# A decoder layer on one core: the second attention of batch 0 moved eight steps later in a written plan

## The reference

```python
x = x + attn(layernorm(x))      # 16 heads of 8, scores + q.rel_emb_k[clip(j-i)], softmax, .(v + rel_emb_v[...])
x = x + xattn(ctx, layernorm(x))  # shifts the sequence by 32 (and by 8), appends ctx and a strided convolution
x = x + ffn(layernorm(x))
# ffn(src): q, k, v (k and v through a rank of 32), rope on q and k, softmax attention, Wo,
#   rmsnorm; a shared SwiGLU MLP of 256, and 8 experts in 2 groups, the best 2 of the best group, gated;
#   out = rmsnorm(x + shared + routed)
```

## Time and profile before

| what | value |
|---|---|
| time, 3 runs | 451.37, 451.47, 452.81 us (median 451.47) |
| the profiled execution | 455.62 us, span 453.8 us |
| mean granted TensorE clock | 0.874 |
| busy PE | 387.8 us (85%) |
| busy DVE | 289.3 us (64%) |
| busy ACT | 236.0 us (52%) |
| busy POOL | 167.7 us (37%) |

### The profile page before, as it was taken

One profiled execution on the slowest core, in us unless ns is written; L12 is line 12 of the kernel. 1 busy time (PEld: TensorE's weight loads), 2 busy tenths in 40 slices (PEclk: granted clock), 3 DMA queues, 4 the chain that ended last, 5 costly groups with the idle time before them and its releaser, 6 DMA issues.

```text
span 453.8 us, 14631 instructions
## 1 busy us (share of the span) xinstructions
PE 387.8 (85%) x6148; PEld 228.1 (50%) x6163; DVE 289.3 (64%) x518; ACT 236.0 (52%) x494; POOL 167.7 (37%) x347
## 2 busy tenths in 40 slices
PE   5967887999999989898988887989788888987973
PEld 5411354666767667565455545544355454543431
DVE  3744765676687778878388878555877820353445
ACT  1533366576667676666652665476157768212200
POOL 5540044454677666474451132120025100013462
PEclk9975555698999999999999968879858988998989
DMA  7300000000000000100003200000000000000000
GB/s 235 100 1 10 13 3 4 4 5 21 6 4 6 6 4 9 26 5 2 3 4 85 72 13 12 2 2 1 2 1 2 5 2 3 0 1 12 0 12 24
DMA packets 12078, 8.19 MB, mean 18 GB/s; under 512 B 4558, under 2 KB 11102, under 8 KB 11886
## 3 DMA queue, kind: packets, MB, share of 16 engines
q1 hardware_dynamic: 12014, 7.27, 5.6%
HBM read 5.94 MB, written 0.52 MB: 14 GB/s over the span
## 4 chain that ended last, share of the span: by engine, by line
PE 57%; DVE 18%; ACT 7%; issue 7%; POOL 5%; SPq 3%; DMA 2%; ACTq 0%; POOLq 0%; DVEq 0%
PE ps L1086 10%; DVE m_qk L808 8%; PE ps L1063 7%; PE ps L1000 7%; PE ps L1019 6%; PE ps L1104 5%; PE ps L1049 5%; ACT arena L656 5%; PE ps L1194 4%; PE ps L1180 4%; PE ps L1159 2%; PE ps L925 2%; SPq L364 2%; PE ps L1110 2%; POOL rstd L413 1%
## 5 line engine op out<-in xcount | busy, mean ns | idle before, releaser
L808 DVE TENSOR_REDUCE m_qk<-ps 128x2 f32<-128x1024 f32 x128 | 153.3, 1219 | 43.1 <-PE ps L1019 42.3
L656 ACT ACTIVATE arena<-ps 128x512 f32<-128x512 f32 x256 | 139.0, 596 | 66.0 <-PE ps L1063 64.7
L1086 PE MATMUL ps<-arena,v_sb 128*20 128x128 f32 x2048 | 84.9, 295 | 0.0
L578 POOL TENSOR_TENSOR arena<-arena,eb 128x256 f32<-128x256 f32 x64 | 47.3, 739 | 63.4 <-ACT arena L656 33.1
L1063 PE MATMUL ps<-q_op,k_op 62*128 62x128 bf16 (+1 forms) x1024 | 56.8, 235 | 14.6 <-ACT arena L656 9.0
L1019 PE MATMUL ps<-k_op,q_op 48*128 48x512 bf16 x256 | 57.2, 443 | 8.2 <-DVE m_qk L808 6.5
L1063 PEld LDWEIGHTS ps<-q_op,k_op 62*128 62x128 bf16 (+1 forms) x1024 | 39.6, 102 | 41.5 <-ACT arena L656 21.0
L1086 PEld LDWEIGHTS ps<-arena,v_sb 128*20 128x20 f32 x2048 | 50.3, 104 | 18.5 <-issue 6.3
L412 POOL TENSOR_SCALAR var<-mv 128x4 f32<-128x4 f32 (+1 forms) x16 | 3.2, 201 | 114.9 <-ACT eb L718 62.9
L643 ACT ACTIVATE eb<-ps 128x512 f32<-128x512 f32 (+1 forms) x64 | 31.3, 541 | 27.1 <-PE ps L1049 26.9
L1000 PE MATMUL ps<-part,sel 32*128 32x512 bf16 x192 | 34.1, 471 | 8.2 <-issue 2.0
(11 more groups left out here) (200 smaller groups left out, 474.3 us busy)
## 6 DMA issues: line engine op xcount, KB each, us to landing
rel_v<-in_relv_ext SPq DMA_DIRECT2D x1, 1024.0 KB, 8.8
eb<-in_w SPq DMA_DIRECT2D x2, 512.0 KB, 6.2
x_sb<-in_x SPq DMA_DIRECT2D x2, 256.0 KB, 3.2
q_op<-farT SPq DMA_DIRECT2D x32, 3.0 KB
q_op<-farT SPq DMA_DIRECT2D x32, 1.5 KB
out<-x_sb SPq DMA_DIRECT2D x8, 64.0 KB, 1.5
rows<-in_rows SPq DMA_DIRECT2D x1, 448.0 KB, 6.6
sel<-in_sel SPq DMA_DIRECT2D x1, 384.0 KB, 4.2
```

The costliest lines, as they stand in the source:

```text
L578: pool.tensor_tensor(on0, on0, eb0[u % 2][:, p], ALU.mult)
L656: act.activation(p_ring[:, k % SLOTS_P, e, :], ps[:, bank, :], ACT.Exp).then_inc(sm["bank_free"], 1)
L808: dve.tensor_reduce(m_qk[:, u % NT, n:H:PAIRS], ps[:, banks, :], AX_X, ALU.max).then_inc(sm["pair_free"], 1)
L1086: i = pe.matmul(out, v_sb[:, IT * b + jt, 4 * g + hh, :], rhs, start=(g == 0 and jt == 0), stop=(u >= NT and jt == IT - 1), skip_group_che ...
```

## The change

Only numbers of the plan change. The four tiles of the second attention of batch 0 begin at 113, 122, 131, 140 and not at 105, 115, 125, 134; those of batch 1 one later each, at 153, 162, 171, 180. `y2` of batch 0 goes from 161.5 to 167.5, that of batch 1 from 206.5 to 207.5. The gate of batch 0 goes from 167 to 173, its two exponentials from 169 and 173 to 175 and 179, and `LAST` from 198.6 to 199.6. The middle stages (`MID_AT` 78 and 126) and `again` stay. No operation is added or removed.

```diff
 MID_AT = (78, 126)
-AGAIN_AT = (105, 115, 125, 134, 152, 161, 170, 179)
-FRONT_AT = (161.5, 206.5)
-LAST = 198.6
+AGAIN_AT = (113, 122, 131, 140, 153, 162, 171, 180)
+FRONT_AT = (167.5, 207.5)
+LAST = 199.6
...
-    plan += [(167, 5, "gate", 0, 0), (169, 5, "group_exp", 0, 0), (173, 5, "expert_exp", 0, 0)]
+    plan += [(173, 5, "gate", 0, 0), (175, 5, "group_exp", 0, 0), (179, 5, "expert_exp", 0, 0)]
```

## The result

The changed kernel is slower: median 469.9 us of four runs (467.4 to 471.3) against 452.1 for the kernel before (451.4 to 453.8), ratio 1.038 [1.032, 1.044]. The forecast was 449.2 with 445 to 454.5; direction and range are wrong. Single runs of any of these kernels differ by some per cent with the clock they got, so every ratio here leaves out the runs that are over some 1.5% longer than the fastest of their kernel, while medians go over all runs.

A forecast was written before the change was run, and what follows sets the result against it. PE was taken as the bound in all stretches but D, where DVE bounds; -2.2 + 3.0 - 1.0 + 0.5 - 2.6 = -2.3 us, or -0.5%, made the median 449.2, range 445 to 454.5.

The forecast's parts named there:

- A: From the end of `again` of batch 0 to `y` of batch 1: fewer maxima there, -2.2 us.
- The allowance of 1.5: In A: 1.5 us charged for a fall of the clock, out of up to 3.4, against a gain of 3.7.
- B: From `y` of batch 1 to its first `again`: four maxima and a `fin` come in on DVE, +3.0 us.
- the 43 to 45: Sign that B is right: the first `again` of batch 1 comes 43 to 45 us behind `y`.
- rival 4: Late shift DMAs make PE wait at `scores` of tile 9: 1 to 2 us, 451; chance inside two other rivals'.
- DVE without a gap over 1 in the last 12: Sign for B: DVE has no gap over 1 us in the last 12 us before the first `again`.
- C: First to last `again` of batch 1: moved `scores` and `pv` fill PE's idle place, clock stays up, -1.0 us.
- D: From the last `again` of batch 1 to `qk_rows` of tile 12: maxima bound by DVE, +0.5 us.
- E: From `qk_rows` of tile 12 to that of tile 13: at full clock 13.3 us instead of 17.14, -3.8.
- F: From `qk_rows` of tile 13 to the first `mlp` of batch 0: takes over `xT` and the gate, +1.2 us.
- Rival 2: Slower, 24%: PE starved between `back` of tile 6 and `y` of batch 1, clock stays low into B; +3.2, 454.7.

The follow-up runs named there:

- the filled hole: The changed kernel with 12 dense filler matmuls on PE ahead of the last maximum of tile 11, where PE idled 3.0 us: 459.4 us, ratio 1.013.

## Why the prediction was wrong

**A, right in size, in part by luck.** -2.15 for -2.2. `back` of tile 6 started at 238.86 behind 2.08 us of PE idle (worked out: 239.5 behind some 2.3). `y` started at 256.37; all of A begins 0.65 earlier here, so that is 1.5 later than the 255.5 worked out without clock loss. The allowance of 1.5 fits, and the clock did fall, at 239.5 for 3.4 us with PE busy in all of them and again at 253. But only the first of the two falls seems to cost A anything. In three other profiles with this order of A the second one is longer, and A takes 28.0 at a clock of 0.83 or 0.84; here and in a fourth it takes 28.2 and 28.3 at 0.88. Where the first one is 6.8 long and not 3.4 (the filled hole), A takes 28.9. How much of the 1.5 is clock and how much DVE, which is busy for 20.2 of A, no run tells.

```profile
238.86 0.33 PE L1118 MATMUL ps<-ident,xn 128*128 128x128 f32 x1 [2.08 <-DVE xn L844]
256.37 2.08 PE L1137 MATMUL ps<-w_out,xnT 128*128 128x128 f32 x8
271.77 0.40 PE L1063 MATMUL ps<-q_op,k_op 50*128 50x128 bf16 x8 [2.49 <-DMA q_op<-neg_mT]
```

**B, right in kind, 1.1 short.** +4.1 for +3.0, within its high end of +4.5: the first `again` 45.1 behind `y`, just past the 43 to 45. The shift DMAs did what the earlier trace rows gave: the rows of tile 9 release `scores` 15.4 behind `y` (estimated 15.1), and PE waits 2.49 there, under the 3 that would have been rival 4. From `y` to DVE's first projection operation it took 31.5, where it had 31.6; the whole growth stands behind that, as forecast, and it isn't the clock, which is 0.88 over B where it was 0.83. But the mark "DVE without a gap over 1 in the last 12" failed:

```profile
293.17 1.22 DVE L808 TENSOR_REDUCE m_qk<-ps 128x2 f32<-128x1024 f32 x1
296.95 1.21 DVE L323 TENSOR_TENSOR rest<-part 128x512 f32<-128x512 f32 x1 [1.43 <-ACT part L696]
```

I had filled DVE's idle time with the maxima as if their order were free. It is a queue: DVE waits for ACT with a maximum ready behind it.

**C, the step that failed.** The step was "the moved `scores` and `pv` of tile 10 now fill that place", for -1.0, with +1.1 as the worst if the clock stays as it was. The place wasn't filled: the idle time ahead of the first `again` grew from 1.96, which is 1.65 without the missing matmul, to 3.00, with another 1.15 just ahead of it. I counted the work that moves in and not the wait of PE that the queue on DVE makes (the pair of `max`, behind the split, behind ACT). And I bounded a fall by the one seen, 6.8 us; it was 37.4. The worst case stood in no bound of mine, and the rows had it: 15.0 busy with 6.3 of it at half clock is 11.9 at full clock, 13.0 with the 1.1 that is added, and 26.0 all at half clock, +10 on the 16.05. +7.1 came. The filled hole puts C at 13.1 at full clock, so my 14.4 for it was even too long.

**D failed for two reasons.** +6.25 for +0.5. It began at half clock: 0.67 over the stretch. And its work was mis-sized: at full clock, in the run with three fillers per `again`, D takes 12.5, where I had 10.3, with PE busy for 11.1 (I had about 9) and DVE for 10.9. At full clock, then, C and D take 25.6 (13.1 and 12.5), and the forecast had 25.4 for them: the two errors of size cancel, and the clock is what made the forecast wrong.

**E and F.** -0.65 for -2.6. E is 15.03 at 0.77 against the 13 to 15 and "over 0.8": the 17.1 us at half clock behind the maxima of tile 12 shrank to 6.8 (from 345.5) but didn't go, so E gained 2.1 of the 3.8 that I counted. F lost 1.46, for 1.2 forecast.

**A reading.** I wrote that PE is the busiest engine in all six stretches but D. In A it is DVE, by a little: 25.87 to 25.73.

**The rivals.** Rival 2 (24%, 454.7) had the sign and the kind: PE starved in a thin place, and a clock that stays low. Its place was wrong: the falls in A and at `y` were 3.4 and 6.8 us, and B kept 0.88. The fall that decides stands 45 us later, where I had written a gain. The rule cited from the Trainium skill, "TensorE: Matmul & The Clock Gate", section "What's actually happening", that throttled is the default and activity releases it, is borne out for the fall (2.35 busy of 6.50). For the release the trace asks for more than the rule says: C has 23.19 us of PE without a pause, at 0.50 throughout.

**What stays open.** Why 1.65 of idle ahead of the first `again`, behind the same work, was followed by a fall of 6.8 us in before, of 20.5 in the kernel without its filler and by none with batch 0's tiles put back; and why executions of one kernel differ (before: 448.8 to 463.5 on one chip, with clocks of 0.89 to 0.85). Which property of the matmuls in `again` keeps the clock down (their 32 rows, the mixture, or something else) wasn't separated.

## What to carry to other kernels

When a plan moves filler, follow the queue of each engine and not its idle total: a ready operation behind one that waits is no filler, and the engine that waits for its buffer starves. Look at what runs *behind* a thin place before pricing a fall of the clock: the price is the length of the stage that doesn't bring it back, and that stage's own fall in the trace of before is no upper bound. A few dummy matmuls exactly in the thin place recovered most of such a loss here (ratio 1.038 to 1.013), and where PE had less idle time than they fill they cost more than they gave (0.994 to 1.007).

## What was new about the hardware

- A stretch at half clock lasted 37.4 us while PE was busy for 33.69 of them, among these 23.19 without a pause. Behind the first 100 us, the low stretches that end inside the span measured about 3.4, 6.8, 10.2, 13.7, 17.1, 20.5, 23.9 or 37.4 us in all these profiles.
- The clock that is still high survives the same stage: C is at 1.00 with PE busy 12.59 of 14.33 (tile 11 two steps earlier), and at 0.50 with PE busy 23.19 of 23.19. So the busy share of a stretch doesn't tell its level.
- Two more matmuls of 128x512 per `again` ended the low stretch after 6.8 us; the same addition over the first picks left it at 61.4, within the 54.6 to 61.4 of the kernels without it.
